# A wavelet convolution with a median filter on one core: products of two images computed in the first stage, TensorE's filler removed, the median's instructions and GpSimd's steps reordered

## The reference

```
a, h, v, d = dwt2(x)                                # 2x2 Haar bands, 16x16 each
proc(c)    = relu(batchnorm(W1 @ c))                # statistics over all 16 images, one set per band
rimg0      = idwt2(proc(a), proc(h), proc(v), proc(d))
rimg1      = x                                      # three levels down and up again: the identity
y  = relu(batchnorm(conv3x3([rimg0, rimg1], W3) + bias))   # 256 -> 128 channels, statistics over all images
out = y + (W2 @ median3x3(y) + b2)                  # 3x3 median with zero padding
```

## Time and profile before

| | before |
|---|---|
| time, median of 3 runs (lowest, highest) | 434.85 us (433.34, 435.02) |
| the profiled execution: its time, its span | 433.21 us, 431.4 us |
| PE busy, instructions | 403.5 us (94%), 1150 |
| DVE busy, instructions | 400.2 us (93%), 532 |
| ACT busy, POOL busy | 148.7 us (34%), 201.6 us (47%) |
| mean of one: POOL's split of x (two per image, L201, L202) | 1.05 us |
| mean of one: ACT's y (L533), squares (L539) | 0.64 us, 0.66 us |
| granted clock of PE over the span | 0.988 of 2.4 GHz |
| chain that ended last, by engine | DVE 71%, PE 23% |

### The profile page before, as it was taken

How to read it: one execution, slowest core, us unless ns; L and a number is a source line. 1 busy time by engine, 2 the same in 40 slices (tenths; PEclk the granted TensorE clock), 3 DMA queues, 4 the chain that set the end, 5 groups by cost and what they waited for, 6 DMA issues and landing times.

```text
span 431.4 us, 3699 instructions
## 1 busy us (share of the span) xinstructions
PE 403.5 (94%) x1150; PEld 212.9 (49%) x1150; DVE 400.2 (93%) x532; ACT 148.7 (34%) x342; POOL 201.6 (47%) x191
## 2 busy tenths in 40 slices
PE   7887999999999999999999999999999969678895
PEld 2333698855444444444444444444455858553332
DVE  3899739999789999999999999999999999999996
ACT  2546742404141322222233314142323312217922
POOL 4999391707181917264453627180826600003630
PEclk9999999999999999999999999999999998969999
DMA  8960200101010101010101001010100000000566
GB/s 306 418 273 1 99 0 2 49 0 47 4 49 0 49 2 49 0 49 0 50 1 49 12 36 50 0 49 0 51 0 0 0 1 2 0 0 0 242 258 281
DMA packets 7652, 26.72 MB, mean 62 GB/s; under 512 B 976, under 2 KB 1232, under 8 KB 7504
## 3 DMA queue, kind: packets, MB, share of 16 engines
q1 hardware_dynamic: 7632, 26.48, 16.0%
HBM read 18.09 MB, written 8.39 MB: 61 GB/s over the span
## 4 chain that ended last, share of the span: by engine, by line
DVE 71%; PE 23%; issue 3%; DMA 1%; ACT 0%; SPq 0%; DVEq 0%
PE conv_ps L359 19%; DVE one_ps L724 4%; DVE sorted_cols L760 4%; DVE one_ps L772 4%; DVE one_ps L774 4%; DVE sorted_cols L768 4%; DVE one_ps L758 4%; DVE z L776 4%; DVE sorted_cols L729 4%; DVE sorted_cols L727 4%; DVE sorted_cols L731 4%; DVE sorted_cols L726 4%; DVE sorted_cols L770 3%; DVE sorted_cols L766 3%; DVE y L854 3%
## 5 line engine op out<-in xcount | busy, mean ns | idle before, releaser
L359 PE MATMUL conv_ps<-ru,wt 128*128 128x512 f32 (+1 forms) x360 | 132.4, 505 | 0.0
L359 PE MATMUL conv_ps<-xu,wt 128*128 128x496 f32 (+3 forms) x240 | 89.8, 512 | 11.5 <-DVE conv_ps L702 11.5
L359 PEld LDWEIGHTS conv_ps<-ru,wt 128*128 128x128 f32 x360 | 69.7, 194 | 53.4 <-issue 49.7
L533 ACT ACTIVATE y<-conv_ps,sgn 128x512 f32<-128x512 f32 (+1 forms) x40 | 25.7, 642 | 185.1 <-PE conv_ps L359 185.1
L278 POOL TENSOR_TENSOR xu<-raw 128x480 f32<-128x480 f32 x16 | 16.7, 1042 | 138.3 <-PE conv_ps L359 138.3
L359 PEld LDWEIGHTS conv_ps<-xu,wt 128*128 128x128 f32 x240 | 46.6, 195 | 48.2 <-issue 33.2
L359 PE MATMUL conv_ps<-y,v 128*128 128x496 f32 (+3 forms) x120 | 43.8, 501 | 1.6 <-ACT wt L486 1.6
L359 PE MATMUL conv_ps<-y,wt 128*128 128x496 f32 (+3 forms) x120 | 43.7, 500 | 0.0
L359 PE MATMUL conv_ps<-ru,v 128*128 128x496 f32 (+3 forms) x120 | 43.7, 500 | 0.0
L341 PE MATMUL one_ps<-y,w 128*128 128x512 f32 x64 | 30.2, 610 | 5.3 <-DVE z L611 3.8
L433 PE MATMUL conv_ps<-z,w 128*128 128x512 f32 x64 | 30.3, 612 | 4.0 <-DVE y L854 4.0
(11 more groups left out here) (124 smaller groups left out, 669.2 us busy)
## 6 DMA issues: line engine op xcount, KB each, us to landing
raw<-x SPq DMA_DIRECT2D x20, 512.0 KB, 3.3
out<-y SPq DMA_DIRECT2D x15, 512.0 KB, 2.7
ru<-x SPq DMA_DIRECT2D x8, 512.0 KB, 8.6
xu<-x SPq DMA_DIRECT2D x4, 512.0 KB, 8.6
wt<-w_t SPq DMA_DIRECT2D x1, 1152.0 KB, 11.3
out<-y SPq DMA_DIRECT2D x2, 256.0 KB, 2.8
w<-w_t SPq DMA_DIRECT2D x2, 64.0 KB, 4.6
vec<-vectors SPq DMA_DIRECT2D x1, 3.0 KB, 9.3
```

The source lines that it names most:

```text
L359: return nc.tensor.matmul(bank(u, b)[:, (r0 - row) * BW:(r1 - row) * BW], taps(half, kx, ky), plane[:, (r0 + dy) * BW:(r1 + dy) * BW], sta ...
L533: S.activation(at(slot(n), row * W + b, [[2, cols]]), src, ACT.Identity, scale=sgn[:, :], accum_out=y_sum[:, part:part + 1]).then_inc(y_ke ...
```

## The change

1. `PRE`: the six products of x of image 4 (unit u6) and image 5 (u7) are computed at the end of the first stage in `one_ps`; ACT copies them over the slots of x in SBUF (`pre_kept`), and, when PE has come to pq(u6) and pq(u7), from there into the PSUM banks (`put_early`); PE then only adds the products of r. DVE's first median waits for the two copies, since it uses `one_ps` as scratch.
2. POOL mixes the taps of x after image 9 instead of all taps after image 15; ACT halves them there; W3 comes in two transfers. Six products of x of image 0 stand between the W1 products of images 10 to 15 (`FILLS`). The bridge is gone.
3. `median`: the same 18 instructions in another order; one of them writes into the image's place in `z` instead of `sorted_cols`. In units of full images the two seeds stand apart, near the end of the median; in the others they stand together after 12 instructions.
4. POOL: for image n it waits until the median of image n-3 has made its last reads of two SBUF operands before the second half (`mids_read`), makes `ru12` and `ru03`, waits until the median of image n-2 has read its rows (`rows_read`), and makes `xu03`.
5. `BN3_AT` 9 becomes 8, and 9 finishes instead of 12 stand between median instructions.

```diff
+    FILLS = {n: 1 for n in range(10, 16)}
+    PRE = (4, 5)
-    BN3_AT, FINISH_AT = 9, (19, 20, 22, 24, 25, 27, 28, 30, 31, 32, 34, 35)
+    BN3_AT, FINISH_AT = 8, (17, 18, 20, 21, 22, 24, 25, 27, 28)
...
             for n in BY_POOL:
                 make_xu12(G, n).then_inc(xu12_by_pool, 1)
+                if n == 9:
+                    mix_taps(X_HALF, 1).then_inc(x_taps_mixed, 1)
+            mix_taps(R_HALF, 2).then_inc(taps_mixed, 1)
...
             for n in range(2, IMAGES):
+                if n > 3:
+                    pool.wait_ge(mids_read, last_unit(n - 3) + 1)
                 pool.wait_ge(bands_normed, n + 1)
                 pool.wait_ge(q_done, last_unit(n - 2) + 1)
                 pool.wait_ge(ru03_made, n - 1)
                 make_ru12(G, n).then_inc(ru12_made, 1)
+                make_ru03(n)
+                pool.wait_ge(rows_read, last_unit(n - 2) + 1)
                 make_xu03(n)
-                make_ru03(n)
...
             for n in range(IMAGES):
                 through_w1(n)
-            pe.wait_ge(taps_halved, 2)
-            for u in range(2):
+                if n == min(FILLS):
+                    pe.wait_ge(taps_halved, 2)
+                for _ in range(FILLS.get(n, 0)):
+                    pq_of_x(*early.pop(0))
+            for u, b, ky in early:
+                pq_of_x(u, b, ky)
+            for i, n in enumerate(PRE):
+                pe.wait_ge(bands_made, IMAGES - 1 + i)
                 for b in range(2):
                     for ky in KY_ORDER:
...
+                        mm = nc.tensor.matmul(one_ps[:, i, b * BANK + r0 * BW:b * BANK + r1 * BW], taps(X_HALF, (None, 1)[b], ky),
+                                              planes(slot(n))[b][:, (r0 + dy) * BW:(r1 + dy) * BW],
+                                              start=ky == KY_ORDER[0], stop=ky == KY_ORDER[-1])
+                mm.then_inc(pre_done, 1)
+            pe.wait_ge(taps_mixed, 1)
-            for _ in range(BRIDGE):
-                nc.tensor.matmul(one_ps[:, 0, 0:BANK], zeros[:, 0:CH], zeros[:, :], start=True, stop=True)
...
             for u in range(2):
                 keep_p(u)
+            for i, n in enumerate(PRE):
+                act.wait_ge(pre_done, i + 1)
+                S.activation(slot(n), one_ps[:, i, :], ACT.Identity).then_inc(pre_kept, 1)
             norm_bands(2)
+            def put_early(u, b):
+                act.wait_ge(squares_summed, 2 * (u - 2) + b + 1)
+                S.activation(conv_ps[:, u % 2, b * BANK:(b + 1) * BANK], slot(n)[:, b * BANK:(b + 1) * BANK],
+                             ACT.Identity).then_inc(pre_put, 1)
...
+                V.tensor_tensor(p2, pair(col_mid, 0), pair(col_mid, 1), ALU.max).then_inc(mids_read, 1)
+                if early is not None:
+                    seed_even(early)
+                    seed_odd(early)
```

More of the change, by code:

```diff
@@ L125, in wavelet_conv_median_kernel @@
         w2_in = sem("w2_in")
-        w3_in = sem("w3_in")
+        w3_in = [sem(f"w3_in{k}") for k in range(2)]
         pads_set = sem("pads_set")
@@ L150, in wavelet_conv_median_kernel @@
         ru03_made = sem("ru03_made")
+        rows_read = sem("rows_read")
+        mids_read = sem("mids_read")
         xu03_made = sem("xu03_made")
@@ L251, in _, with mix_taps @@
             G.memset(at(eo[:, :], ODD, [[UP, H]]), 0.0).then_inc(pads_set, 1)
+            def mix_taps(half, count):
+                pool.wait_ge(w3_in[half], 16)
+                row = [[KX * CH, KY], [1, CH]]
+                left, mid, right = (at(wt[:, :], (half * KY * KX + kx) * CH, row) for kx in range(KX))
+                dense = [[CH, KY], [1, CH]]
+                outer = at(outer_taps, half * KY * CH, dense)
+                G.tensor_tensor(outer, left, right, ALU.add).then_inc(outer_summed, 1)
+                pool.wait_ge(outer_summed, count)
+                G.tensor_tensor(at(v1[:, :], half * KY * CH, dense), mid, outer, ALU.add).then_inc(v1_mixed, 1)
+                pool.wait_ge(v1_mixed, count)
+                return G.tensor_tensor(mid, mid, outer, ALU.subtract)
             for n in BY_POOL:
@@ L370, in pq_of_r @@
                 plane = planes(ru12[UNITS[u][0] % 2][:, :])[b]
+                onto = UNITS[u][0] in PRE
                 for ky in KY_ORDER:
-                    mm = product(u, b, R_HALF, (None, 1)[b], plane, ky, stop=ky == KY_ORDER[-1])
+                    mm = product(u, b, R_HALF, (None, 1)[b], plane, ky, stop=ky == KY_ORDER[-1] and not onto, onto=onto)
                 mm.then_inc(done, 1)
@@ L701, in seed, with seed_odd, median @@
                 V.tensor_tensor(p_bank, p_kept[u % 2][:, 0:cols], q_bank, ALU.add)
+            def seed_odd(u):
+                cols = UNITS[u][2] * BW
+                q_bank = conv_ps[:, u % 2, BANK:BANK + cols]
                 V.tensor_tensor(q_bank, p_kept[u % 2][:, 0:cols], q_bank, ALU.subtract).then_inc(seeded, 1)
-            def median(n, kept, pair0=0, pairs=BH, step=step):
+            def median(n, kept, pair0=0, pairs=BH, step=step, seeds=None):
+                early, late = (seeds, None) if n in HALVED else (None, seeds)
                 r0, nr = 2 * pair0, 2 * pairs
@@ L815, in _ @@
             dve.wait_ge(pads_set, 1)
+            dve.wait_ge(pre_kept, len(PRE))
             for u in range(len(UNITS) - 2):
-                medians(PIECES[u:u + 1], seeding(u + 2))
+                medians(PIECES[u:u + 1], seeds=u + 2)
             def second_batch_norm():
```

99 lines of the change are left out of this document (51 added, 48 removed).

## The result

The changed kernel takes 422.0 us (median of 4 runs, 420.67 to 423.78), the one before 434.71 us beside it (433.34 to 435.02, 4 runs). The ratio is 0.9715 with a 95% interval of 0.9677 to 0.9753. The forecast of 421 us holds, and most of its steps are found where it put them. One term is far off: the third stage. That the total is so close is partly luck, as the part on the prediction shows.

What follows compares the result with a forecast made beforehand. PE was taken to set the pace in the middle, DVE the end. 374.8 + 42.5 + 0.5 = 417.8 us span, 419.6 time, 13.6 below the profiled 433.21; against the median 434.85 this gives 421, range 416 to 429.

Steps and rivals of the forecast that it cites:

- the third stage: From the second batch norm to the end: 42.47 us of the same work, +0.5 us taken, ends -1 and +2.5.
- First stage: Stage before the products of r: +1.1 us, ends 0 and +3, from fills and POOL's and ACT's earlier tap steps.
- PE in the middle: Second stage: pq(6) and pq(7) lose six products each, 10.08 us in all; outputs(14) ends at 312.2.
- The wait for `ru12` of image 6: PE in the second stage: smallest margin, 1 to 3 us; if missed, a cost of 1 to 2 us once.
- one of my own signs of being wrong: List of what the new profile would show if the forecast failed; PE waiting for POOL's `ru12` was on it.
- DVE in the middle: Full medians of the second stage: reordering removes six dependent neighbours, 19.17 to 18.42 us; u14's median starts at 313.3.
- no collision while DVE lags: Full medians: POOL's 7.9 us of steps just fit the median's remaining 8.0 while DVE lags PE by some 4 us.
- reordering saves by itself: DVE's median: 0.12 us saved per dependent neighbour; the rival that reordering saves nothing gave 424 us, chance 0.11.
- that rival: DVE and POOL still collide, twice per image (20.4 us): u14 at 325.7, 433 to 434 us; no change by either road 0.06.
- one fixed collision of 1.0 us: Earlier kernel's full median: DVE's first two instructions lose 1.0 us while POOL runs; without it 19.17 instead of 20.17 us.
- The end of the second stage: u15 to u17 and the stretch behind them: second batch norm starts at 374.8 instead of 388.93.
- PE's gap: PE idle 7 us before outputs(17), where it was 4.88, then a lowered clock; claimed to cost nothing, margin 1.8 us.

Runs made afterwards that it cites:

- the best kernel: The changed kernel with 12 finishes instead of 9, and POOL's second half of ru03 waiting until DVE has read the median's rows: 418.22 us.
- the six waits: The changed kernel with six median instructions waiting for the instruction directly ahead instead of the one before that, none moved: 427.24 us.
- its old order: The changed kernel with POOL's steps ordered ru12, xu03, ru03 and without its two waits for the median's progress: 431.39 us.
- The slowed PE: The changed kernel with POOL's earlier step order, without its two waits, plus four products of zeros per image on PE from u4 to u15: 435.25 us.
- 12 places: The changed kernel with 12 finishes instead of 9 between median instructions, three more at instructions 29, 30 and 31: 419.79 us.

## Why the prediction was right, and where it was off

*First stage.* The forecast was +1.1 us for the sums of r and +0.7 for PE, whose first product of r was to come at 54.3; the sums were there 1.6 us later than before (52.2), PE was at 54.81. POOL's three steps on half the columns took 0.99 to 1.00 us each, as taken, near half of the full ones. The two copies of ACT did not cost the up to 0.5 us that I had allowed for them, and this made up for PE's late start: outputs(4) ended at 120.58, forecast 120.54.

*PE in the middle.* The 10.08 us came off; outputs(14) ended 0.9 us later than forecast. The wait for `ru12` of image 6, which I had called a margin of 1 to 3 us, cost 0.6 of it (0.34 us idle, and slower instructions at both of its ends); it was one of my own signs of being wrong. Four of PE's instructions for the two units with early products came 0.07 to 0.09 us late each. Taking the early products away cost 9.5 us by the medians of the runs, 8.3 by the start of u14.

*DVE in the middle.* The reordered median at 18.38 (forecast 18.42) and "no collision while DVE lags" held from the second full median on. The first one collided; I had not counted it. DVE made that good by waiting less later, but POOL's release moved with it, and this is what made PE wait for `ru12`: without the collision, in the best kernel, the wait is gone. That reordering saves by itself is shown by the six waits. That POOL's waits are needed is shown by its old order: that rival has 431.4 us, below the 433 to 434 I gave it, with u14 at 322.0 instead of 325.7.

*A reading that was incomplete.* I read from the earlier trace rows that "PE sets the pace in the middle, DVE follows some us behind". DVE had no wait and took 20.17 us, and I explained the equal times by one fixed collision of 1.0 us. The slowed PE shows that in kernels with POOL's old order the collision is what adapts. For the kernel before itself this is inferred: it has the same order, the same equality and no waits, but no run changed its pace. Its trace speaks for it. The medians of u4 to u6 took 21.12, 21.68 and 21.03 us, DVE fell from 1.1 to 4.4 us behind PE, and from there on each took 20.17 to 20.18 us at that same distance. The conclusion that PE's time must go down was not hurt by it. But it means that less work on PE alone, or fewer collisions alone, gives 3 us, not the 10 that either seemed to be worth.

*The end of the second stage.* Forecast 374.8, measured 375.00. Part of this is luck: u14 started 0.9 us late, and its median was 0.5 us shorter than I had counted, since its seeds are those of a half unit. PE's gap (6.23 us) and lowered clock (2.87, 2.71 and 1.84 us for three groups) cost nothing, but only just: the last squares were there at 374.57, 0.4 us before DVE asked, where I had 1.8.

*Third stage.* This is the term that was mis-sized: +0.5 us taken (ends -1 and +2.5), +3.9 in the profiled run (46.34 against 42.47). I had counted three more finishes at 0.5 us each beside two gains. What the runs show instead: PE stands 2.13 us first, since no finish is placed between the last four median instructions; then seven finishes go at PE's pace; and its clock falls. With 12 places the term is +0.3 (42.8). The changed kernel's runs at 420.7 and 420.8 us have a granted clock of 0.990 and 0.989, those at 423.2 and 423.8 of 0.987 and 0.983. That the clock at the end makes this difference fits the 1.7 us above, but it is not shown: only the run at 423.23 has a trace.

*The total.* For the profiled execution I had 417.8 us of span and 419.6 of time; it has 421.3 and 423.23. So of the 13.6 us forecast, 10.0 are found there, and the missing 3.6 are nearly all the third stage. The forecast of 421 for the median came from setting the same 13.6 us against the median of before, 1.6 us above its profiled execution. The one of the changed kernel lies high among its own, 1.2 us above their median. That the two medians differ by 12.7 us, and 421 is missed by 1.0 only, owes something to this and is no better proof of the working than the rows are.

## What to carry to other kernels

Two engines with the same time per item and no waits are no proof that one of them simply follows: a third engine that starts at the events of the first can stretch the second until the paces agree. Then relief on either engine alone shows little, and both are to be changed together. When instructions of a tail are interleaved with another loop, leave no stretch without one: TensorE waits there, and its clock may be lowered behind the pause.

## What was not expected of the hardware

- The wait for the direct neighbour costs 0.12 to 0.13 us per instruction of DVE even where the one ahead is an independent one (19.17 against 18.38 us for six of them).
- The pause of 2.13 us on PE in the third stage was followed by a lowered clock in five kernels (0.68 in the changed one's window) and by 1.00 in two, the one with six more waits and the one with the slowed PE. The latter has the same pauses just ahead as the changed kernel, so these do not tell the cases apart. After 2.42 us the next groups took 1.82, 2.71 and 1.61 us instead of 1.43, after 7.45 us 2.85 and 2.01.
- Where DVE and POOL both read two SBUF operands, both get longer: 1.76 and 1.71 us for instructions of 0.69 and 1.28.
